# A two-layer spiking and gated network on one core: the recurrence's product written over its PSUM bank, and new instruction orders for all engines

## The chip, the cores and the metric

The kernel runs on one core of a Trainium2 chip. A core has five engines that matter here, each with its own queue that it works off strictly in order: TensorE (PE, matrix products into PSUM), VectorE (DVE), ScalarE (ACT), GpSimd (POOL) and SyncE (SP, which issues the transfers). They meet only at semaphores. The metric is the device time of one execution in microseconds. Three runs of the kernel before gave 676.83, 680.20 and 680.25 us; the median is 680.2.

## The reference

The input `x` has 32 sequences of 256 tokens with 128 channels. Cut to what matters:

```python
def _L0_attn_ref(x, ...):
    x = x + lif(time_mix(layer_norm(x, ln1_s, ln1_b), ...))        # spikes after a recurrence over time
    x = x + lif(channel_mix(layer_norm(x, ln2_s, ln2_b), ...))     # spikes after a gated relu-square layer
    return x

def wkv(w_decay, u, k, v):                                         # inside time_mix
    def step(carry, kv_t):
        ...
        y = (A * p + Bc * vt) / (A * q + Bc)
        return ((A2 * p + B2 * vt, A2 * q + B2, no2), y)

def _L0_ffn_ref(x, ...):
    h = silu(tlin(x, w1)) * tlin(x, w2)
    h = gelu(tlin(h, h1)); h = gelu(tlin(h, h2))
    return tlin(h, w3)

x = x + _layernorm(_L0_attn_ref(_layernorm(x), ...))
x = x + _layernorm(_L0_ffn_ref(_layernorm(x), ...))
```

## The kernel before

The 32 sequences are worked in 16 groups of two, so a group has 512 tokens. Most of the work is on tiles of 128 partitions by 512 values: channels on partitions, the tokens of a group along them. A group passes five sections.

1. Normalise, transpose (`turn_1`, `z_1`), subtract the token before (`shift_1` on GpSimd), blend three inputs (`mix_1`), multiply by Wk, Wv and Wr (`k_product` into bank `p_k`, `v_product` into `p_v`, `r_product_1` into `p_m[0]`). The recurrence is done with scans on VectorE: `maximum` (running maximum over `p_k`), `excess`, `bounds`, exponentials on ScalarE, then `terms(1)` = B2 * v and `sum_over_time(0)` (the scan of p), `sum_over_time(1)` (the scan of q), `weighted_sum` on GpSimd, `denominator`, `numerator`, and `log`, `inverse`, `ratio`, `ratio_end`. `out_product` multiplies by Wo.
2. Spikes: `fire(0)` compares with the threshold and counts, `fired_sum(0)` sums the count on TensorE, `fired_flag(0)` on VectorE copies it out, and `neurons(0)` on GpSimd steps the neurons one by one only where the flag is not zero. `spikes_turned(0)` transposes the spikes back.
3. The channel section: `norm_2`, `turn_2`, `z_2`, `shift_2`, `mix_2`, products `r_product`, `channel_k`, relu, square, `channel_v`, then `neuron_input_2`, `fire(1)`, `fired_flag(1)`, `neurons(1)`, `spikes_turned(1)`, `residual_3`.
4. The gated layer: `norm_4`, `turn_4`, `f0`, four `to_gate` and four `to_value` products with SiLU and `swiglu`, two `hidden` layers of sixteen block products each with `gelu`, and `last_product`. Every activation of this layer is split in a high part (`high` on ScalarE) and a remainder (`low` on VectorE or GpSimd), and each block is multiplied twice.
5. `output_scaled`, `turn_5`, `output_tokens`, a last normalisation (`variance(5)`, `norm_5`) and `residual_5` on GpSimd, and the store.

Five groups are in flight at a time. The program of each engine is written out as turns: in turn i the group i is normalised for the first time, i-1 is in the recurrence, i-2 in its spikes and the channel section, i-3 behind it, i-4 in the gated layer. Three hand-written orders per engine (`first_turn`, `turn`, `last_turn`) are called for turns by `schedule`. TensorE's program is written twice, for weights whose remainder is zero and for others; the choice, a branch on a value loaded from memory, comes after the first turns, behind `channel_k` of the first group. The weights' high parts and remainders (`high_weights`, `low_weights`, `rest_weights`, `rest_max`, `rest_sum`, `rest_flag`) are made in the opening.

PSUM has eight banks: `p_turn` for all transposes, `p_spk`, `p_k`, `p_v`, two `p_m`, two `p_f`. `p_v` takes the v product and two of the four gate products (`to_gate` 1 and 3). TensorE waits, with `after`, until the readers of a bank are done. The lines of the recurrence that the change touches are, before:

```python
dve.tensor_tensor(flat(bv[:, n]), flat(factors[:, 2 + n]), p_v[:, :], ALU.mult).then_inc(s_bv[n], 1)   # terms
new = factors[:, 3] if n else bv[:, 1]                                                                  # sum_over_time
dve.tensor_tensor_scan(pq[:, n, b, 1:T + 1], factors[:, 1, b], new[:, b], 0.0, ALU.mult, ALU.add)
after(pe, s_bv[0], g.n + 2)      # to_gate, m == 1
after(pe, s_bv[1], g.n + 2)
```

## Time and profile before

| | us |
|---|---|
| median of three runs | 680.2 |
| profiled execution | 681.2 |
| its span on the core | 679.1 |
| TensorE busy | 589.6 (87%) |
| VectorE busy | 550.5 (81%) |
| ScalarE busy | 537.6 (79%) |
| GpSimd busy | 439.8 (65%) |

All durations come from the one profiled execution. TensorE's busy time is modelled: matmuls overlap, and the pitch of a row of them is shorter than the time that each is shown with. Idle time of an engine that is waited for by nobody costs nothing, so the shares alone decide nothing: the kernel has an opening in which no engine is full, twelve turns in which TensorE is busy nearly all the time, and an end. The reading below goes by these stretches, then by the waits of one engine, then by single rows.

### The profile page before, as it was taken

How to read it: one execution, taken by the hardware profiler on the slowest of the kernel's cores; microseconds unless marked ns; L12 is line 12 of the kernel's file. 1: busy time of each engine (PE TensorE's matmuls, PEld its weight loads, DVE VectorE, ACT ScalarE, POOL GpSimd, SP SyncE). 2: the span in 40 equal slices, each digit the busy share in tenths (PEclk: the TensorE clock that was granted, in tenths of full speed). 3: DMA queues.
4: the chain of work that ended last, by engine and by line, in shares of the span. 5: the costliest groups of instructions: out<-in, count | busy, mean ns of one | idle time of the engine just before them, and what ended most of it. 6: DMA issues, size and time to landing. Idle time of an engine off the chain costs nothing. (4 is left out here: it accounts for less than half of the span.)

```text
span 679.1 us, 10282 instructions
## 1 busy us (share of the span) xinstructions
PE 589.6 (87%) x2241; PEld 365.0 (54%) x2241; DVE 550.5 (81%) x1532; ACT 537.6 (79%) x849; POOL 439.8 (65%) x576
## 2 busy tenths in 40 slices
PE   1247579999999999999999999999999999989883
PEld 0022236566565657565666656565756566656562
DVE  2865768989898998989898989899898989775631
ACT  4846367998989797979799898979797979858672
POOL 4323454687868686876878786868687784744452
PEclk9857779999999999999999999999999999999997
DMA  6100010001010100101010101010010101000000
GB/s 221 62 18 17 0 32 17 16 17 32 15 33 16 32 0 17 32 17 32 16 33 16 32 18 31 17 32 1 18 31 1 33 0 32 17 0 17 1 16 15
DMA packets 26560, 17.05 MB, mean 25 GB/s; under 512 B 1152, under 2 KB 25728, under 8 KB 26240
## 3 DMA queue, kind: packets, MB, share of 16 engines
q1 hardware_dynamic: 26496, 16.34, 8.0%
q8 instruction: 23, 0.38, 0.2%
q14 instruction: 41, 0.34, 0.2%
HBM read 12.14 MB, written 4.19 MB: 24 GB/s over the span
## 5 line engine op out<-in xcount | busy, mean ns | idle before, releaser
L774 ACT ACTIVATE hid<-p_f,scale 128x512 f32<-128x512 f32 x128 | 88.0, 688 | 64.5 <-PE p_f L1715 64.1
L1715 PE MATMUL p_f<-a_lo,w_hi 128*128 128x512 f32 x320 | 133.1, 416 | 2.8 <-DVE a_lo L293 1.7
L1715 PE MATMUL p_f<-a_hi,w_hi 128*128 128x512 f32 x320 | 125.9, 393 | 0.0
L1715 PE MATMUL p_f<-b_lo,w_hi 128*128 128x512 f32 x256 | 111.8, 437 | 3.5 <-DVE b_lo L293 2.3
L1715 PE MATMUL p_f<-b_hi,w_hi 128*128 128x512 f32 x256 | 100.6, 393 | 0.0
L421 POOL TENSOR_TENSOR rstd<-var,minus_half 128x4 f32<-128x4 f32 x64 | 91.0, 1422 | 2.5
L768 ACT ACTIVATE a_hi<-hid 128x512 fp32r<-128x512 f32 x128 | 79.1, 628 | 2.9 <-DVE hid L1254 1.5
L437 POOL TENSOR_TENSOR nd<-factors,pq 128x512 f32<-128x512 f32 x32 | 39.3, 1229 | 58.6 <-DVE pq L1121 58.6
L293 DVE TENSOR_TENSOR a_lo<-hid,a_hi 128x512 fp32r<-128x512 f32 x96 | 63.8, 689 | 11.2 <-ACT a_hi L768 10.9
L1715 PEld LDWEIGHTS p_f<-a_lo,w_hi 128*128 128x128 f32 x320 | 60.3, 188 | 22.5 <-issue 8.1
L293 POOL TENSOR_TENSOR b_lo<-hid,b_hi 128x512 fp32r<-128x512 f32 x32 | 46.8, 1478 | 34.2 <-ACT b_hi L768 29.4
L1700 PE MATMUL p_m<-kk,mix 128*128 128x512 f32 x128 | 64.1, 607 | 3.6 <-issue 3.6
L1684 PE MATMUL p_m<-mixed,mix 128*128 128x512 f32 x128 | 65.3, 613 | 1.5 <-DVE kk L1200 1.5
L1715 PEld LDWEIGHTS p_f<-a_hi,w_hi 128*128 128x128 f32 x320 | 60.3, 189 | 9.9 <-issue 0.5
L1715 PEld LDWEIGHTS p_f<-b_lo,w_hi 128*128 128x128 f32 x256 | 48.0, 188 | 30.6 <-issue 20.2
L408 POOL TENSOR_TENSOR var<-mv,eps_row 128x4 f32<-128x4 f32 x64 | 23.0, 359 | 58.3 <-DVE mv L1049 58.2
L1715 PEld LDWEIGHTS p_f<-b_hi,w_hi 128*128 128x128 f32 x256 | 48.2, 188 | 13.0 <-issue 3.1
L1521 PE MATMUL p_turn<-ident,n 128*128 128x128 f32 x192 | 32.2, 293 | 25.0 <-ACT n L657 12.2
L1521 PEld LDWEIGHTS p_turn<-ident,n 128*128 128x128 f32 x192 | 22.9, 147 | 54.3 <-DVE n L1064 25.0
L1715 PE MATMUL p_f<-f_lo,w_hi 128*128 128x512 f32 x64 | 39.9, 623 | 8.5 <-ACT gate L755 7.1
L293 POOL TENSOR_TENSOR a_lo<-hid,a_hi 128x512 fp32r<-128x512 f32 x32 | 41.8, 1305 | 7.7 <-ACT a_hi L768 7.7
L511 POOL TENSOR_SCALAR f_out<-f_out,rstd,shift 128x128 f32<-128x128 f32 x64 | 43.2, 689 | 0.2 <-POOL shift L503 0.2
(141 smaller groups left out, 1457.3 us busy)
## 6 DMA issues: line engine op xcount, KB each, us to landing
xa<-in_x SPq DMA_DIRECT2D x16, 256.0 KB, 2.8
xb<-in_x SPq DMA_DIRECT2D x16, 256.0 KB, 2.9
out<-y_out SPq DMA_DIRECT2D x16, 256.0 KB, 3.3
kk<-in_ffn SPq DMA_DIRECT2D x1, 1024.0 KB, 7.6
hid<-in_ffn SPq DMA_DIRECT2D x1, 1024.0 KB, 10.0
mix<-in_mix SPq DMA_DIRECT2D x1, 512.0 KB, 6.3
gate<-in_ffn SPq DMA_DIRECT2D x1, 512.0 KB, 4.5
mix<-in_mix SPq DMA_DIRECT2D x1, 320.0 KB, 3.9
```

The costliest lines, as they stand in the source:

```text
L293: eng.tensor_tensor(lo[:, m], hid[:, m], hi[:, m].bitcast(F32), ALU.subtract).then_inc(s_lo[layer][m], 1)
L408: pool.tensor_tensor(var[n][:, :], mv[n][:, :, 1], eps_row[:, :], ALU.add).then_inc(s_var[n], 1)
L421: pool.tensor_tensor(rstds[n][:, :], var[n][:, :], minus_half[:, 0], ALU.pow).then_inc(s_rstd[n], 1)
L437: pool.tensor_tensor(nd[:, n], factors[:, 0], pq[:, n, :, 0:T], ALU.mult).then_inc(s_apq, 1)
L511: last = pool.tensor_scalar(f_out[:, j], f_out[:, j], rstd5[:, j:j + 1], shift5[:, j:j + 1], ALU.mult, ALU.add)
L768: act.activation(dst[:, m], hid[:, m], ACT.Copy).then_inc(s_hi[layer], 1)
L774: act.activation(hid[:, m], p_f[m % 2][:, :], ACT.Gelu, scale=scale[:, 1 + layer, m:m + 1]).then_inc(s_gelu[layer], 1)
L1521: last = pe.transpose(p_turn[:, j * P:(j + 1) * P], tiles[:, j], ident[:, :])
L1684: pe.matmul(p_m[m % 2][:, :], mix[:, MIX["fWk"] + m], flat(mixed2[:, 1]), start=True, stop=True).then_inc(s_fk, 1)
L1700: last = pe.matmul(p_m[0][:, :], mix[:, MIX["fWv"] + m], kk[:, m], start=(m == 0), stop=(m == HB - 1))
L1715: last = pe.matmul(out_, w[:, b], x[:, k], start=(k == 0 and t == 0), stop=(k == n - 1 and t == len(terms) - 1))
```

## The change

Two things change. First, `terms(1)` writes its product over the values of `p_v` in PSUM, and `sum_over_time(0)` scans from there; `bv` keeps only the product of `terms(0)`. `terms(0)` has to come before `terms(1)` now, which a wait enforces. Second, the orders of all engines are laid anew: per engine one `opening` (up to the first groups' gated layer), one `turn` that is looped for i = 5 to 12, and one `ending`, each a plain list of steps. TensorE's waits on banks stand in these lists between the steps, no longer inside the steps, and its branch on the weights comes between `opening` and `onset`. The steps themselves are the same.

```diff
@@ terms
+                if n == 1:
+                    dve.wait_ge(s_bv[0], g.n + 1)
-                dve.tensor_tensor(flat(bv[:, n]), flat(factors[:, 2 + n]), p_v[:, :], ALU.mult).then_inc(s_bv[n], 1)
+                dve.tensor_tensor(p_v[:, :] if n else flat(bv[:, :, :]), flat(factors[:, 2 + n]), p_v[:, :], ALU.mult).then_inc(s_bv[n], 1)
@@ sum_over_time
-                new = factors[:, 3] if n else bv[:, 1]
+                new = factors[:, 3] if n else p_v[:, :].rearrange("p (b t) -> p b t", b=NB)
@@ numerator
-                dve.tensor_tensor(nd[:, 0], nd[:, 0], bv[:, 0], ALU.add).then_inc(s_num, 1)
+                dve.tensor_tensor(nd[:, 0], nd[:, 0], bv[:, :, :], ALU.add).then_inc(s_num, 1)
@@ all engines
-            schedule(first_turn, turn, last_turn)
+            opening()
+            for i in range(FIRST, LAST + 1):
+                turn(groups(i))
+            ending()
@@ tensor, the looped turn
+                    after(pe, s_f_cm, g[4].n)
+                    to_gate(g[3], 0)
+                    after(pe, s_f0_hi, g[3].n)
+                    after(pe, s_f0_lo, g[3].n)
+                    turn_5(g[4])
...
+                    after(pe, s_pq, g[1].n, 2, 2)
+                    to_gate(g[3], 1)
@@ gpsimd, the looped turn
+                shift_1(g[0])
+                norm_5(g[4])
+                neurons(1, g[2])
+                neurons(0, g[1])
```

VectorE in an even turn, around the two copies of the spike counts (`fired_all1` of the older group, `fired_all0` of the younger; `mixed1` is `mix_1`, `spikes` is `fire`, `b_lo` is `low(2)`). Before:

```order
L1206 SCALAR_TENSOR_TENSOR h_in1<-tanh_r2,p_m0 128x512
L293 TENSOR_TENSOR a_lo<-hid,a_hi 128x512 x2
L1155 TENSOR_SCALAR spikes1,fired1<-h_in1 128x512
L1162 COPY fired_all1<-p_m0 1x1
L1155 TENSOR_SCALAR spikes0,fired0<-p_k 128x512
L1080 SCALAR_TENSOR_TENSOR mixed1<-d1,vec,z1 128x512
L1162 COPY fired_all0<-p_m0 1x1
L1212 TENSOR_TENSOR x3<-p_spk,x2 128x512
```

The same place now:

```order
L1590 SCALAR_TENSOR_TENSOR h_in1<-tanh_r2,p_m0 128x512
L1539 TENSOR_SCALAR spikes0,fired0<-p_k 128x512
L1539 TENSOR_SCALAR spikes1,fired1<-h_in1 128x512
L1462 SCALAR_TENSOR_TENSOR mixed1<-d1,vec,z1 128x512
L1546 COPY fired_all1<-p_m0 1x1
L1431 BN_AGGR mv1<-bn1 128x2 x4
L1462 SCALAR_TENSOR_TENSOR mixed1<-d1,vec,z1 128x512 x2
L287 TENSOR_TENSOR b_lo<-hid,b_hi 128x512
L1546 COPY fired_all0<-p_m0 1x1
L1596 TENSOR_TENSOR x3<-p_spk,x2 128x512
```

The younger group's `fire` and all three `mix_1` now stand ahead of or between the two copies, with `moments_1` and a `low(2)`.

ScalarE in the opening, first group (`w_rest` marks the passes over the weights' remainders, `y<-nd` is `log`, `y<-y` is `inverse`). Before:

```order
L704 ACTIVATE factors<-factors 128x1024
L643 ACTIVATE w_hi<-gate 128x1024
L649 ACTIVATE kk,w_rest<-w_lo 128x2048
L643 ACTIVATE w_hi<-f_cm 128x512
L649 ACTIVATE hid,w_rest<-w_lo 128x2048
L649 ACTIVATE gate,w_rest<-w_lo 128x1024
L649 ACTIVATE f_cm,w_rest<-w_lo 128x512
L710 ACTIVATE y<-nd 128x512
L714 ACTIVATE y<-y 128x512
L657 ACTIVATE n1<-xa,nmr1,rstd1 128x128 x4
```

The same place now:

```order
L832 ACTIVATE factors<-factors 128x1024
L829 ACTIVATE factors<-factors 128x1024
L785 ACTIVATE n1<-xa,nmr1,rstd1 128x128 x4
L838 ACTIVATE y<-nd 128x512
L842 ACTIVATE y<-y 128x512
L777 ACTIVATE hid,w_rest<-w_lo 128x2048
L794 ACTIVATE z1<-p_turn,vec 128x2x256
L848 ACTIVATE h_in0<-p_k 128x512
L777 ACTIVATE kk,w_rest<-w_lo 128x2048
```

The passes over the remainders moved behind `inverse`, and the second group's `norm_1` (`n1`) ahead of `log`.

ScalarE at the last group (`f_cm` is `output_scaled` and `f_out` is `output_tokens` of the group before, `gate` is SiLU). Before:

```order
L747 ACTIVATE f0_hi<-p_turn 128x512
L782 ACTIVATE f_cm<-p_f0,vec 128x512
L787 ACTIVATE f_out<-p_turn 128x512
L693 ACT_TABLE_LOAD
L755 ACTIVATE gate<-p_f0,scale 128x512
```

The same place now:

```order
L875 ACTIVATE f0_hi<-p_turn 128x512
L821 ACT_TABLE_LOAD
L910 ACTIVATE f_cm<-p_f0,vec 128x512
L883 ACTIVATE gate<-p_f0,scale 128x512
```

The table load moved ahead of `output_scaled`, and `output_tokens` behind the SiLU steps.

## Rows read from the trace of the kernel before

**Rows 1.** Stretches: length; busy PE, PEld, DVE, ACT, POOL; clock; DMA; GB/s

```profile
0.00:99.45 99.45, 47.67 (x98) 19.41 (x98) 62.70 (x166) 53.73 (x77) 38.39 (x69) 0.74 0.18 60
...
320.52:357.26 36.74, 35.55 (x142) 22.45 (x140) 33.56 (x96) 32.28 (x53) 27.98 (x36) 1.00 0.08 23
...
541.00:578.79 37.79, 35.93 (x142) 22.50 (x141) 33.77 (x90) 32.75 (x53) 25.05 (x31) 1.00 0.05 15
...
642.30:679.10 36.80, 22.31 (x90) 15.42 (x88) 10.87 (x28) 19.14 (x28) 15.61 (x24) 0.87 0.05 15
```

**Rows 2.** Waits of PE, ten turns from 136.64: us in total, times, longest

```profile
PE p_f L1715 <- ACT gate L755: 4.5, 10, 0.5
PE p_m L1646 <- DVE mixed L1192: 3.2, 10, 0.3
PE p_turn L1521 <- DVE n L1064: 2.1, 10, 0.2
```

**Rows 3.** Waits of DVE in the same ten turns

```profile
DVE fired_all L1162 <- PE p_m L1616: 25.8, 20, 2.2
```

**Rows 4.** Timeline of DVE in one turn: start, us, operation, [idle before]

```profile
331.94 0.15 DVE L1162 COPY fired_all<-p_m 1x1 f32<-1x1 f32 x1 [2.16 <-PE p_m L1616]
...
342.29 0.75 DVE L1080 SCALAR_TENSOR_TENSOR mixed<-d,vec,z 128x512 f32<-128x512 f32 x1
...
347.02 1.29 DVE L293 TENSOR_TENSOR a_lo<-hid,a_hi 128x512 fp32r<-128x512 f32 x2
...
349.60 1.67 DVE L1064 TENSOR_SCALAR n<-xres,mv,rstd 128x128 f32<-128x128 f32 x4
```

**Rows 5.** Groups of DVE by form: count, busy us, mean ns

```profile
L1110 DVE TENSOR_TENSOR bv<-factors,p_v 128x512 f32<-128x512 f32 x32 | 21.3, 666 | 0.0
L1121 DVE TENSOR_TENSOR_SCAN pq<-factors,bv 128x256 f32<-128x256 f32 x32 | 20.3, 675 | 0.0
...
L1087 DVE TENSOR_TENSOR_SCAN o<-decay_row,p_k 128x256 f32<-128x256 f32 x32 | 19.7, 659 | 1.2 <-PE p_k L1555 1.2
```

**Rows 6.** Timelines of DVE, ACT and PE in the opening

```profile
31.28 0.69 DVE L1128 TENSOR_TENSOR nd<-nd,factors 128x512 f32<-128x512 f32 x1 [0.55 <-POOL nd L437]
...
70.13 0.69 DVE L1206 SCALAR_TENSOR_TENSOR h_in<-tanh_r,p_m 128x512 f32<-128x512 f32 x1 [2.94 <-PE p_m L1700]
...
34.45 0.61 ACT L710 ACTIVATE y<-nd 128x512 f32<-128x512 f32 x1
...
37.13 2.05 PE L1595 MATMUL p_k<-yr,mix 128*128 128x512 f32 x2 [2.05 <-issue]
...
42.52 0.61 PE L1632 MATMUL p_spk<-ident,spikes 128*128 128x128 bf16 x4 [2.29 <-POOLq L476]
...
64.72 5.37 PE L1700 MATMUL p_m<-kk,mix 128*128 128x512 f32 x8 [3.59 <-issue]
...
96.71 0.47 PE L1715 MATMUL p_f<-f_lo,w_hi 128*128 128x512 f32 x1 [1.34 <-DVE f_lo L1243]
```

**Rows 7.** Timeline at the last group

```profile
641.75 0.39 PE L1715 MATMUL p_f<-f_hi,w_hi 128*128 128x512 f32 x1
...
642.32 1.28 ACT L693 ACT_TABLE_LOAD   x1
...
643.61 0.69 ACT L755 ACTIVATE gate<-p_f,scale 128x512 f32<-128x512 f32 x1
...
648.39 0.48 PE L1715 MATMUL p_f<-a_lo,w_hi 128*128 128x512 f32 x1 [1.02 <-POOL a_lo L293]
```

**Rows 8.** Timelines of POOL, ACT and PE around the spikes of one turn

```profile
327.91 2.81 POOL L511 TENSOR_SCALAR f_out<-f_out,rstd,shift 128x128 f32<-128x128 f32 x4
330.69 1.04 POOL L442 TENSOR_TENSOR d<-z 128x512 f32<-128x512 f32 x1
...
328.28 0.76 ACT L666 ACTIVATE z<-p_turn,vec 128x512 f32<-128x512 f32 x1
...
333.72 0.38 PE L1632 MATMUL p_spk<-ident,spikes 128*128 128x128 bf16 x4
```

More of the change, by code:

```diff
@@ L1003, in _ @@
+            opening()
+            for i in range(FIRST, LAST + 1):
+                turn(groups(i))
+            ending()
         @block.vector
@@ L1513, in _ @@
+            opening()
+            for i in range(FIRST, LAST + 1):
+                turn(groups(i))
+            ending()
         @block.tensor
@@ L1516, in _, with program @@
             pe.wait_ge(s_vec, 4)
-            def program(general, **turns):
+            def program(general, first):
                 def turned(n, g, tiles):
@@ L2063, in _ @@
+                if first:
+                    opening()
+                else:
+                    onset()
+                    for i in range(FIRST, LAST + 1):
+                        turn(groups(i))
+                    ending()
+            program(False, True)
             for k in range(len(parts)):
```

2829 lines of the change are left out of this document (1848 added, 981 removed).

## Prediction

> **What bounds the kernel now.** I read first the busy time by stretch, then the waits of one engine at a time inside the even stretch, then the timelines at the places where a wait sits. The stretches are cut at the load of the SiLU table, which ScalarE makes once per group. [rows 1] show three parts: an opening of 99.45 us until the first of them, with TensorE busy 47.67 us at a mean granted clock of 0.74; twelve even turns, of which one stands there (36.74 us; TensorE 35.55, VectorE 33.56, ScalarE 32.28, GpSimd 27.98 busy); and 138.1 us behind 541.00, of which the first turn takes 37.79 and the last group alone 36.80, with TensorE busy for 22.31 of them. In an even turn TensorE bounds: it is idle 1.19 us, VectorE 3.18, ScalarE 4.46. [rows 2] say where TensorE's 1.19 go, over ten turns: 4.5 us for the SiLU gate, 3.2 us for `mix_2`, 2.1 us for the normalised tokens of `norm_4`, so 0.98 a turn out of 1.19. Two of these three are VectorE's lateness. Yet VectorE itself stands still 2.58 us a turn at `fired_flag`, for a sum on TensorE [rows 3]; most of it is one gap of 2.16 us [rows 4]. VectorE waits early in the turn and is late at its end: that can be mended by order alone. The opening and the end are bound by chains of single steps, not by any engine's work.
>
> **The arithmetic of the recurrence.** `terms(1)` writes its product into the PSUM bank instead of SBUF, and the two scans of `sum_over_time(0)` read it there. No instruction is added or removed: per group one 128x512 product and two 128x256 scans change an operand. The product with an operand already in PSUM takes 666 ns, the scan with both operands in SBUF 675, the scan with one in PSUM (the `maximum` scan of `p_k`) 659 [rows 5]. The nearest row therefore gives -16 ns a scan, 32 x 16 ns = 0.5 us in all; a VectorE write into PSUM has no row here. From below, 0.5 us gained; from above, if product and scans each became slower by what separates a `mix_1` (0.75 us [rows 4]) from this product, about 80 ns x 48 = 3.8 us. I take nought, because the scan row with PSUM is the nearest.
> [...]
> The bank `p_v` now stays taken until the scan ends (`to_gate(1)` waits for `s_pq`, no longer for `s_bv`). Before, the order was scan then `terms(0)`; now both products precede the scan. In either order the last of the same instructions frees the bank, so this costs nothing; if the scan were last by a whole product more, 0.66 us a turn.
>
> **The even turns.** TensorE's order hardly moves: the output transposes go behind the first gate product, one `channel_v` goes behind the value products. What moves is VectorE's. Into the gap at `fired_flag(1)` come `fire(0)` and one `mix_1`, and between the two flags `moments_1`, two more `mix_1` and a `low(2)`. So 2 x 0.74 us of `mix_1` leave the path from the `maximum` scan to `mix_2`, and one `low(3)` (half of the 1.29 us pair) goes from before `norm_4` to behind it [rows 4]. I walked the new order through one turn with these durations: `mix_2` can come only as early as `z_2` and `shift_2` allow, about 0.3 us earlier than now; `norm_4`, which starts at 349.60, is free some 0.8 us earlier; then ScalarE, which runs without a gap from `z_2` to `output_scaled`, becomes what the first gate product waits for. The walk gives a turn between 35.1 and 36.1, depending on how the short ScalarE gaps round. Bounds: nothing gained, if ScalarE takes over at once, and 1.19 us, if every idle moment of TensorE went. I take 0.65, somewhat over half of the ceiling and the late end of the walk: 12 x 0.65 = 7.8 us, bounds 0 and 14.3.
>
> **The opening.** Four steps. (a) `log` of the first group ran at 34.45, with four passes over the weights' remainders ahead of it on ScalarE; the denominator that it needs was complete at 31.97 [rows 6]. The passes now stand behind `inverse`. That is 2.5 us, and `stats_1` of the next group no longer holds up the first `mix_1` (0.9 us): the out product goes from 37.13 to about 33.7. (b) TensorE then stood 2.29 us for the spikes at 42.52 [rows 6], since GpSimd had the next group's `shift_1` ahead of `neurons`, and that waited for `z_1`. The transposes and `z_1` of that group now come before the out product: 2.3 us. (c) In front of the channel products TensorE stood 3.59 us on its own instruction stream, at the branch on the weights [rows 6]. The branch moves to behind the first `turn_4`. Here I count 1 us, as the squares on ScalarE are late there too; the new place costs up to 3.6 us at the first gate product. (d) Between `neuron_input_2` at 70.13 and the first gate product at 96.71 [rows 6] the new order brings `norm_4` of the first group ahead of work for the third: some 5 us, of which (c) takes back 3.6. In all 3.4 + 2.3 + 1 + 5 - 3.6 is 8.1; I take 7.2, because one new wait (the weights' maximum sits on TensorE before `v_product`) may hold 1 us. Bounds: 2.5, if only (a) holds, and 11, if the branch hides behind other waits.
>
> **The end.** For the last group the first gate product was ready at 642.14, but SiLU began at 643.61 behind the table load at 642.32 [rows 7]. Now the table is loaded ahead of `output_scaled`, and `turn_5` of the group before goes behind the gate products: 1.5 to 1.9 us. GpSimd's `low(1)` then stood behind the variance of the group before, and TensorE waited 1.02 us for it [rows 7]; it now stands ahead. Together 2.4 us at the last group. The three stretches before it have the same pattern with shorter waits; I take 1.6 us for all three. Sum 4.0, bounds 0 and 7.
>
> **The sum.** The profiled execution took 681.2 us (span 679.1). 681.2 - 7.8 - 7.2 - 4.0 = 662.2. It lies 1.0 us above the median of the runs, 680.2, so on the median the forecast is 661.2. With all lower bounds 681.2 - 0 - 2.5 - 0 - 1.0 = 677.7; with all upper ones 681.2 - 14.3 - 11 - 7 - 1.0 = 647.9.
>
> **Rivals.** *ScalarE takes over.* The turn stays at 36.74, as ScalarE's run up to `output_scaled` is the new chain; opening and end keep their gain: 680.2 - 7.2 - 4.0 = 669.0. For it: ScalarE has 32.28 us in a turn [rows 1] and waits only for products. Against: two of TensorE's waits are for VectorE [rows 2]. Chance 0.2.
> *The orders buy nothing measurable.* The opening's gain is given back as a wait of the second and third group, whose steps were moved behind the first's, and the even turns are as long as before: only the end is left, 680.2 - 2.4 = 677.8. Within 0.5% (676.8 to 683.6), which is about what a measurement of this kernel can tell from no change. For it: the twelve turns set the pace whatever starts earlier. Chance 0.1.
> *Slower: GpSimd between `shift_1` and `neurons`.* `norm_5` now stands directly ahead of `neurons(1)`, and TensorE needs the spikes in order. `z_1` ends at 329.04, `shift_1` takes 1.04, `norm_5` took 2.81 beside VectorE [rows 8]: 332.9, and the spike transposes are due at 333.72, so 0.8 us are left for `neurons`. The four `norm_5` instructions now run beside `fire` and `mix_1` of VectorE. If each is held for a 0.75 us instruction, four take 4.8 us and the turn grows by 2.0: 680.2 - 7.2 - 4.0 + 12 x 2.0 = 693. It decides the sign from 0.93 us a turn (11.2 / 12). Against: in the even turn before, 2.81 us were stretched already, and the transposes waited on GpSimd nowhere there [rows 2]. Chance 0.08.
> [...]
>
> **How the numbers follow.** Forecast 661.2 with its neighbourhood (648 to 668): 0.62. ScalarE takes over, 669.0: 0.2. Nothing measurable, 677.8: 0.1. Slower, 693: 0.08. The range goes from 649 to 677: it takes in the forecast, the first rival and nearly all of the sum's bounds. Faster by over 0.5% is forecast and first rival, 0.82; within 0.5% 0.1; slower 0.08.
>
> **What would show it.** Right: the first SiLU table load near 92 us instead of 99.45; even turns of 36.1; `fired_flag`'s wait under 1 us a turn; scans on `p_v` at 0.66 us; the last SiLU directly behind its gate product. Wrong: a wait of TensorE for the spikes on GpSimd in each turn, a wait of the first gate product for the scan of `p_v`, product or scans on `p_v` above 0.75 us, or a first table load later than 97 us.

## The result: 671.0 us, and the profile of the changed kernel

The changed kernel took 671.03 us in the median of four runs (669.68 to 673.51), the kernel before 678.52 us on the same chip: a ratio of 0.9895, 95% interval 0.9847 to 0.9942. It is faster by about 1%, and the time lies inside the range, but the gain is 7.5 us where 19 were forecast. The profiled execution is the slowest of the four (673.5 us, span 671.6), so stretches below are compared trace with trace: 679.1 before, 671.6 after.

The stretches, cut as in [rows 1] at the load of the SiLU table (columns as there; two even turns stand here, because there are two kinds now):

```profile
0.00:89.48 89.48, 43.65 (x94) 17.54 (x95) 64.07 (x171) 53.52 (x77) 43.14 (x72) 0.81 0.20 66
202.01:239.52 37.51, 35.52 (x142) 22.58 (x140) 34.88 (x96) 32.35 (x52) 24.11 (x35) 1.00 0.07 22
277.05:313.55 36.50, 35.51 (x142) 22.59 (x140) 34.00 (x96) 32.37 (x52) 24.55 (x35) 1.00 0.08 23
537.76:574.99 37.23, 35.34 (x143) 22.71 (x141) 34.69 (x89) 32.57 (x54) 20.63 (x27) 1.00 0.05 15
633.34:671.60 38.26, 24.48 (x102) 17.12 (x100) 11.70 (x30) 20.03 (x30) 15.25 (x25) 0.89 0.05 14
```

The opening fell from 99.45 to 89.48 us (-9.97, forecast -7.2), the part from the thirteenth table load on from 138.1 to 133.84 (-4.3, forecast -4.0). The twelve even turns between them grew from 441.55 to 448.28 us: +6.7 where -7.8 were forecast. That is more than the whole miss: opening and end together gained 3 us more than forecast. (The last table load is no clean cut any more: it now comes ahead of the first gate product, as planned.)

Eight of the twelve turns belong to the looped order; these are looked at from here on. Their table loads lie at 173.36 and 467.49 before (294.1 us, 36.77 each) and at 164.50 and 461.99 after (297.5 us). They give 3.4 of the 6.7 us; the two turns ahead of them grew by 1.1 us and the two behind them by 2.3, and these four belong to the written-out opening and end. Five of the eight take 37.5 us, three 36.5 to 36.8. TensorE's busy time is the same in both kinds (35.5), VectorE's is not: 34.88 against 34.00, with the same 96 instructions.

The waits of TensorE over these eight turns (us in total, times, longest):

```profile
PE p_f L2233 <- DVE b_lo L287: 5.5, 5, 1.1
PE p_v L2233 <- DVE pq L1505: 2.9, 8, 0.4
PE p_f L2233 <- DVE hid L1638: 2.3, 8, 0.5
PE p_m L2202 <- DVE mixed L1576: 1.3, 8, 0.2
```

The waits of [rows 2] for the gate and for `norm_4` are gone. In their place stand three waits for VectorE: 1.1 us for `low(2)` (`b_lo`) in exactly the five long turns, 0.36 us in each turn for the scan of `p_v` ahead of the second gate product, 0.29 us for `swiglu` (`hid`). VectorE's own wait of [rows 3] has gone as intended, from 2.58 to 0.29 us a turn:

```profile
DVE fired_all L1546 <- PE p_m L2186: 2.3, 8, 0.3
```

The forms of VectorE that answer to [rows 5] (count, busy us, mean ns, idle before), and `low(2)`:

```profile
L287 DVE TENSOR_TENSOR b_lo<-hid,b_hi 128x512 fp32r<-128x512 f32 x32 | 28.2, 882 | 9.7 <-ACT b_hi L896 9.7
...
L1505 DVE TENSOR_TENSOR_SCAN pq<-factors,p_v 128x256 f32<-128x256 f32 x32 | 20.2, 674 | 1.6
...
L1494 DVE TENSOR_TENSOR p_v<-factors,p_v 128x512 f32<-128x512 f32 x16 | 11.1, 692 | 1.3
...
L1494 DVE TENSOR_TENSOR bv<-factors,p_v 128x512 f32<-128x512 f32 x16 | 10.8, 678 | 0.0
```

The scan takes 674 ns from PSUM as it took 675 from SBUF, the product into the bank 692 instead of 666 to 678. `b_lo` went from 679 ns in the kernel before to 882. Its rows in a long turn (first three lines) and in a short one (last two), from the timelines of GpSimd, VectorE and TensorE (start, us, operation, [idle before]):

```profile
219.55 1.32 POOL L507 TENSOR_TENSOR y_out<-f_out,xres 128x512 f32<-128x512 f32 x1
...
219.59 1.83 DVE L287 TENSOR_TENSOR b_lo<-hid,b_hi 128x512 fp32r<-128x512 f32 x1
...
221.56 0.48 PE L2233 MATMUL p_f<-b_lo,w_hi 128*128 128x512 f32 x1 [1.10 <-DVE b_lo L287]
...
294.65 0.81 DVE L287 TENSOR_TENSOR b_lo<-hid,b_hi 128x512 fp32r<-128x512 f32 x1
...
294.86 1.75 POOL L507 TENSOR_TENSOR y_out<-f_out,xres 128x512 f32<-128x512 f32 x1
```

In the long turn GpSimd's `residual_5` (`y_out`) starts 0.04 us before VectorE's `low(2,3)`; the latter then takes 1.83 us, which is the 1.28 us that `residual_5` still runs and some 0.55 of its own. In the short turn `low(2,3)` starts first, and `residual_5` takes 1.75 us. Which of the two goes first decides whether TensorE waits 1.1 us. At a distance of 0.02 us the recorded starts do not tell which it will be: in the turns with `residual_5` at 182.08 and 257.12 it leads by 0.02 us and goes first, and at 443.03, in the last of the eight turns, it leads by as much, but `low(2,3)` goes first (0.67 us) and `residual_5` takes 1.86 us.

### The profile page after: what moved, and what is told of

It is laid out like the page before. It is cut to its first block and busy times, and to the rows that moved or that the text cites. A ratio compares the mean times of both kernels' runs of the same rounds, so it can differ in the third digit from the quotient of the medians.

```text
span 671.6 us, 9752 instructions
## 1 busy us (share of the span) xinstructions
PE 585.3 (87%) x2241; PEld 365.9 (54%) x2241; DVE 561.4 (84%) x1532; ACT 537.4 (80%) x849; POOL 401.7 (60%) x576
## 5 line engine op out<-in xcount | busy, mean ns | idle before, releaser
L287 DVE TENSOR_TENSOR a_lo<-hid,a_hi 128x512 fp32r<-128x512 f32 x96 | 65.8, 705 | 8.7 <-ACT a_hi L896 7.8
L410 POOL TENSOR_TENSOR rstd<-var,minus_half 128x4 f32<-128x4 f32 x64 | 69.3, 1087 | 1.6
L287 POOL TENSOR_TENSOR a_lo<-hid,a_hi 128x512 fp32r<-128x512 f32 x32 | 49.4, 1544 | 33.2 <-ACT a_hi L896 33.0
L287 POOL TENSOR_TENSOR b_lo<-hid,b_hi 128x512 fp32r<-128x512 f32 x32 | 42.3, 1323 | 37.8 <-DVE fired_all L1546 23.5
L2142 PE MATMUL p_turn<-ident,n 128*128 128x128 f32 x192 | 30.6, 284 | 29.1 <-ACT n L785 21.0
L1462 DVE SCALAR_TENSOR_TENSOR mixed<-d,vec,z 128x512 f32<-128x512 f32 x48 | 35.8, 768 | 11.7 <-POOL d L431 11.7
L397 POOL TENSOR_TENSOR var<-mv,eps_row 128x4 f32<-128x4 f32 x64 | 15.4, 246 | 48.1 <-DVE mv L1431 48.1
L418 POOL TENSOR_SCALAR x<-xa,neg_mean,rstd 128x128 f32<-128x128 f32 x64 | 40.0, 637 | 0.2 <-POOL rstd L406 0.2
```

What stands on the lines that cost most here:

```text
L287: eng.tensor_tensor(lo[:, m], hid[:, m], hi[:, m].bitcast(F32), ALU.subtract).then_inc(s_lo[layer][m], 1)
L397: pool.tensor_tensor(var[n][:, :], mv[n][:, :, 1], eps_row[:, :], ALU.add).then_inc(s_var[n], 1)
L410: pool.tensor_tensor(rstds[n][:, :], var[n][:, :], minus_half[:, 0], ALU.pow).then_inc(s_rstd[n], 1)
L418: last = pool.tensor_scalar(out_[:, j], in_[:, j], neg_mean[n][:, j:j + 1], rstd[:, j:j + 1], ALU.add, ALU.mult)
L1462: dve.scalar_tensor_tensor(mixed1[:, n], d1[:, :, :], col(("tmk", "tmv", "tmr")[n]), z1[:, :, 0:T], ALU.mult, ALU.add).then_inc(s_mixed1, 1)
L2142: last = pe.transpose(p_turn[:, j * P:(j + 1) * P], tiles[:, j], ident[:, :])
```

## The experiments

Two questions: do the long turns come from this collision, and why does a turn without it still take 36.5 us where the walk gave 36.1. Times are medians; a ratio stands with its 95% interval, against the kernel before on the same chip (678.5 us for the changed kernel, 679.7 to 680.1 us for the others). "Eight turns" are the looped ones, in the one profiled execution of each run. The runs x8 to x10, x13, x14, x18 and x19 leave out parts of the work, so that their output is not the layer's; they serve only to find what bounds a turn.

| run | time, us | ratio to before | eight turns, us |
|---|---|---|---|
| before | 678.5 | | 294.1 |
| changed | 671.0 | 0.9895 (0.9847 to 0.9942) | 297.5 |
| x5_yield | 667.6 | 0.9828 (0.9801 to 0.9855) | 291.8 |
| x6_collide | 692.3 | 1.0192 (1.0167 to 1.0217) | 302.4 |
| x2_resid | 679.3 | 0.9998 (0.9985 to 1.0010) | 303.3 |
| x4_arith | 684.7 | 1.0072 (1.0048 to 1.0095) | 296.9 |
| x1_sbuf | 672.8 | 0.9911 (0.9884 to 0.9938) | 295.2 |
| x7_yield_sbuf | 669.8 | 0.9871 (0.9843 to 0.9898) | 291.8 |
| x3_both | 683.2 | 1.0060 (1.0039 to 1.0082) | 304.8 |
| x8_less_act | 666.1 | 0.9809 (0.9777 to 0.9840) | 291.8 |
| x9_less_dve | 667.8 | 0.9830 (0.9796 to 0.9864) | 291.6 |
| x10_sbuf_less_act | 668.7 | 0.9851 (0.9816 to 0.9886) | 291.7 |
| x13_less_both | 665.7 | 0.9794 (0.9780 to 0.9808) | 291.4 |
| x14_less_pool | 666.8 | 0.9818 (0.9791 to 0.9844) | 291.8 |
| x18_all | 664.7 | 0.9796 (0.9751 to 0.9842) | 291.2 |
| x19_den | 664.1 | 0.9788 (0.9742 to 0.9834) | 289.4 |
| x15_late5 | 676.7 | 0.9943 (0.9929 to 0.9958) | 300.3 |
| x16_late5_sbuf | 678.0 | 0.9979 (0.9967 to 0.9990) | 300.1 |
| x11_two_yields | 667.5 | 0.9829 (0.9803 to 0.9854) | 291.7 |
| x12_log_late | 671.9 | 0.9894 (0.9864 to 0.9925) | 295.2 |

### The collision, taken out and put in

**x5_yield.** `residual_5` lets `low(2,3)` go first:

```diff
@@ changed kernel, GpSimd, looped turn
                 low(2, g[3], 2)
+                pool.wait_ge(s_lo[2][3], g[3].n + 1)
                 residual_5(g[4])
```

> The changed kernel with one wait more in GpSimd's even turn: residual_5 keeps its place, but begins only when low(2,3) of VectorE is done. Theory of the collision (who comes first at the SBUF decides, and in five of eight turns residual_5 came first by some 40 ns): low(2,3) takes 0.7 to 0.8 us in every turn, TensorE's wait of 1.1 us for it is gone, and residual_5, which took 1.75 us in the short turns because it waited itself, ends where it ended in those. No turn of 37.5 us is left among the eight, they take 292.5 us instead of 297.5, and the whole time is 666 instead of 671. Rival (GpSimd's chain behind residual_5 is the bound, as x2_resid hints, where its delay came back as a wait for weighted_sum): the eight turns take 303 and the whole 677 or more.

667.62 us, and all runs between 667.35 and 667.88. TensorE's wait for `b_lo` is no longer among its waits over the eight turns, and no turn of 37.5 us is left among them. First the waits, then the form of VectorE:

```profile
PE p_v L2234 <- DVE pq L1506: 2.9, 8, 0.4
PE p_f L2234 <- DVE hid L1639: 2.3, 8, 0.5
PE p_m L2203 <- DVE mixed L1577: 1.3, 8, 0.2
```

```profile
L287 DVE TENSOR_TENSOR b_lo<-hid,b_hi 128x512 fp32r<-128x512 f32 x32 | 22.5, 703 | 9.5 <-ACT b_hi L897 9.5
```

The eight turns fall by 5.7 us, the expected 5. An added wait made the kernel faster: this version beats both kernels, by 3.4 us the changed one.

**x6_collide.** The reverse: in the kernel before, only this line of GpSimd's order goes where the change put it.

```diff
@@ kernel before, GpSimd, turn
                 if on[0]:
                     shift_1(g[0])
-                if on[4]:
-                    residual_5(g[4])
...
                     low(2, g[3], 2)
+                if on[4]:
+                    residual_5(g[4])
```

> The kernel before with one line of GpSimd's even turn moved as the change moved it: residual_5 from ahead of neurons to behind low(2,2). In the kernel before, low(2,2) ends at 337.81 and low(2,3) of VectorE begins at 337.93, so residual_5 would come first by 0.1 us. Theory of the collision: low(2,3) grows from 0.67 to about 1.8 us, TensorE waits about 1.1 us for it, a turn grows from 36.75 to 37.3 to 37.8 us, and the whole time by 6 to 12 us to 685 to 691. Rival (the collision needs the other moves of the change too, or is hidden): 679 +- 1.5, and low(2,3) as before.

692.33 us; each looped turn grows by 1.03 us. The form of `b_lo` has 1063 ns on the mean over all 32 instructions instead of 679, and TensorE waits 1.1 us for it in each of the eight turns:

```profile
L293 DVE TENSOR_TENSOR b_lo<-hid,b_hi 128x512 fp32r<-128x512 f32 x32 | 34.0, 1063 | 7.8 <-ACT b_hi L768 7.8
```

```profile
PE p_f L1715 <- DVE b_lo L293: 8.8, 8, 1.1
```

So the move of one GpSimd instruction to where it meets `low(2,3)` costs 12.5 us, and the collision is shown from both sides.

**x2_resid.** Moving `residual_5` further back instead of letting it wait:

```diff
@@ changed kernel, GpSimd, looped turn
-                residual_5(g[4])
                 variance(2, g[1])
                 variance(3, g[2])
                 rstd(2, g[1])
+                residual_5(g[4])
                 rstd(3, g[2])
```

> The changed kernel with one line of GpSimd's even turn moved: residual_5 stands behind rstd(2) instead of directly behind low(2,2). Theory of the collision (in the long turns residual_5 of GpSimd starts some 40 ns before low(2,3) of VectorE, which then takes 1.83 us instead of 0.68, and TensorE waits 1.1 us for it): low(2,3) takes 0.7 us in each turn, TensorE's wait of 1.1 us for it is gone, the five long turns of 37.5 us become 36.5 us, eight turns take 292.5 us instead of 297.5, the whole 666 instead of 671. Rival (the long turns come from the spikes' flag, which GpSimd waits for ahead of low(2,0), or from VectorE's amount of work): low(2,3) stays long or another of VectorE's instructions gets long in its place, turns of 37.5 stay, 671 +- 1.

679.31 us, 8 us slower than the changed kernel. The collision with `low(2,3)` was gone (`b_lo` 703 ns), but GpSimd ran later, and an instruction of 0.20 us (`neg_mean`) came beside three VectorE instructions with two SBUF inputs in a row and took 1.92 us. Its row on GpSimd, and the wait of TensorE that came of it over the eight turns:

```profile
308.76 1.92 POOL L399 TENSOR_TENSOR neg_mean<-mv,minus_one 128x4 f32<-128x4 f32 x1
```

```profile
PE p_v L2233 <- DVE pq L1505: 11.7, 8, 1.6
```

The expectation was right on the place and wrong on the time: the collision had moved to a dearer place.

### The arithmetic and the bank

**x4_arith.** The new arithmetic alone, in the old orders:

```diff
@@ kernel before, with the change's terms, sum_over_time and numerator; VectorE, turn
+                    terms(g[1], 0)
                     terms(g[1], 1)
                     denominator(g[1])
                     sum_over_time(g[1], 0)
-                    terms(g[1], 0)
```

> The kernel before with the new arithmetic alone: the second product is written over p_v and scanned there, the first product goes ahead of it, and TensorE waits for the scan where it waited for the products; all other orders are those of before. If the arithmetic is worth nought, as predicted: the time of before, 678.5 +- 1.5, turns of 36.75 us, scans of 0.67 us; in the old order a product stood behind the scans, so the bank is released no later than before. Rival (PSUM costs VectorE time): product or scans above 0.75 us, up to 3.8 us more in all. Rival (the bank): a wait of TensorE for the scan takes the place of the 0.45 us wait for the gate, and the turn grows by what the scan is later.

684.70 us, 4.9 us more than the kernel before, a turn 37.1 instead of 36.77. The instructions cost what was forecast (product 696 and 670 ns, scan 671), yet a turn is 0.34 us longer, since the product that must now go first pushes `denominator` back: ScalarE waits 0.24 us a turn for it, which it did not before, and TensorE's wait for the gate [rows 2] grows from 0.45 to 0.80 us. Over eight turns, ScalarE and TensorE:

```profile
ACT y L710 <- DVE nd L1130: 1.9, 8, 0.2
```

```profile
PE p_f L1715 <- ACT gate L755: 6.4, 8, 0.8
```

The changed kernel escapes this: its order has `denominator` ahead of both products.

**x1_sbuf** and **x7_yield_sbuf**: the old arithmetic in the new orders, without and with the added wait of x5_yield.

```diff
@@ changed kernel, terms and sum_over_time as before the change; TensorE, all orders
-                    after(pe, s_pq, g[1].n, 2, 2)
+                    after(pe, s_bv[1], g[1].n)
                     to_gate(g[3], 1)
```

> The changed kernel with the old arithmetic: the second product goes to SBUF again and is scanned from there, and the second gate product waits for the two products on the bank, no longer for the scan. Theory of the bank (the bank p_v is held for two scans, 1.26 us, longer than it need be, and TensorE pays 0.36 us of that in each turn): the wait of TensorE for the scan of p_v (0.4 us a turn in the changed kernel) is gone, an undisturbed turn falls from 36.5 to about 36.1, and the whole time by 12 x 0.36 = 4 us, from 671 to 667. Rival (ScalarE takes over): the same 0.4 us come back as a wait for the SiLU gate, as in the kernel before, and the time stays at 671 +- 1. Rival (the product into PSUM and the scans from it are slower): product 692 -> 670 ns, scans 674 -> 675 ns, 0.4 us in all.

> x5_yield with the old arithmetic (second product to SBUF, bank released by the products). x1_sbuf showed short turns of 36.4 to 36.6 us, TensorE's wait for the scan replaced by waits for the gate and for swiglu. If ScalarE's run up to the gate bounds an undisturbed turn, the eight turns take 291.5 to 292.5 us and the time is that of x5_yield within 1.5 us. If the bank bounds it, 4 us less than x5_yield.

x1_sbuf took 672.8 us, so the 4 us of the bank did not come; three of its eight turns are long by the collision. The wait for the scan goes, and in its place come waits for `swiglu` and for the gate; without the collision the eight turns are 291.8 us with and without the early release. TensorE in x7_yield_sbuf:

```profile
PE p_f L2234 <- DVE hid L1639: 3.0, 8, 0.6
PE p_f L2234 <- ACT gate L884: 2.2, 8, 0.3
```

So the bank is not what holds the turn. The time is 2.2 us above x5_yield, all of it outside the looped turns: the first table load is 1.1 us later (90.88 against 89.79), the end 0.8 us longer. In these orders a scan from SBUF takes 728 ns on the mean, from PSUM 674 (the form of x1_sbuf):

```profile
L1505 DVE TENSOR_TENSOR_SCAN pq<-factors,bv 128x256 f32<-128x256 f32 x32 | 21.9, 728 | 1.6
```

The 54 ns are no price of each scan. In x1_sbuf a pair of scans takes 1.26 to 1.28 us, but for three pairs of 2.20, 1.74 and 1.44 us, and beside each of these three GpSimd has an instruction; they make 1.6 of the 1.7 us that 32 scans lost. The first of the three, VectorE and GpSimd in x1_sbuf, and the same place of VectorE in the changed kernel, where the same GpSimd instruction starts at 28.35 and the scans are not held:

```profile
28.26 2.20 DVE L1505 TENSOR_TENSOR_SCAN pq<-factors,bv 128x256 f32<-128x256 f32 x2
28.30 1.61 POOL L426 TENSOR_TENSOR nd<-factors,pq 128x512 f32<-128x512 f32 x1 [1.45 <-DVE pq L1505]
...
28.30 1.26 DVE L1505 TENSOR_TENSOR_SCAN pq<-factors,p_v 128x256 f32<-128x256 f32 x2
```

**x3_both** is x1_sbuf and x2_resid together.

> Both edits at once: old arithmetic with the bank released by the products, and residual_5 behind rstd(2). If both theories hold and their gains lie at different places of the turn, a turn takes about 36.1 us, eight turns 289, and the whole time is 671 - 5 - 4 = 662, which is the forecast of the prediction. If only the collision counts 666, if only the bank 667; if neither 671.

683.22 us. With the bank released early the 1.46 us a turn of x2_resid turn up chiefly as a wait for the gate of ScalarE (7.6 us in eight turns), since `log` waits for the late `denominator`. Neither gain showed.

### What holds a turn without the collision

The rival of the prediction was that ScalarE takes over. **x8_less_act** takes work from ScalarE behind the exponentials, **x9_less_dve** from VectorE ahead of the scans, **x10_sbuf_less_act** joins x7 and x8.

```diff
@@ x5_yield, ScalarE (x8_less_act): output_scaled, f0, output_tokens
-                act.activation(f_cm[:, 0], p_f[0][:, :], ACT.Copy, scale=col("w3_s"))
+                act.activation(f_cm[:, 0, 0:64], p_f[0][:, 0:64], ACT.Copy, scale=col("w3_s"))
...
@@ x5_yield, split_low (x9_less_dve)
+            n = 64 if layer == 3 and m else N
-            eng.tensor_tensor(lo[:, m], hid[:, m], hi[:, m].bitcast(F32), ALU.subtract)
+            eng.tensor_tensor(lo[:, m, 0:n], hid[:, m, 0:n], hi[:, m, 0:n].bitcast(F32), ALU.subtract)
```

> x5_yield with less work on ScalarE: output_scaled and f0 do 64 of 512 columns, output_tokens 128 of 512, from the second group on; the output is not the layer's. That is some 1.1 us a turn in the run that ends in the SiLU gate. If ScalarE's run bounds an undisturbed turn, it falls from 36.5 to between 35.6 and 36.0 us and the eight turns to 285 to 288. If VectorE or the bank bounds it, turns stay at 36.5 and the wait of TensorE for the scan of p_v stays at 0.4 us.

> x5_yield with less work on VectorE: low(3,1), low(3,2) and low(3,3) do 64 of 512 columns; the output is not the layer's. That is some 1.6 us a turn, at the end of VectorE's run ahead of the scans and the gate. If VectorE's run bounds an undisturbed turn (x8_less_act left it at 36.47 us with 1.1 us less on ScalarE, and the wait for the scan of p_v stayed), the turn falls to between 35.7 and 36.1 us, the eight turns from 291.8 to 286 to 289, and TensorE's wait of 0.4 us for the scan of p_v is gone. Rival (ScalarE and VectorE end together, so that taking work from one shows the other): at most 0.1 us a turn, 291 for the eight, and a wait for the gate in place of that for the scan.

> x7_yield_sbuf (bank released by the products) with the reduced work on ScalarE of x8_less_act; the output is not the layer's. In x7 the wait for the scan was replaced by waits for the gate (0.3 us) and for swiglu (0.4 us), in x8 it stayed. If the bank and ScalarE's run end within 0.1 us of each other and both must go, the turn falls here from 36.47 to about 36.1 us and the eight turns to 289. If VectorE's run is the bound whatever the bank and ScalarE do, 36.4 to 36.5 us and a wait for swiglu of VectorE remains.

None of the three moved the turn: 291.8, 291.6, 291.7 us. ScalarE therefore is not the bound by its amount of work, and the rival falls; nor is VectorE ahead of the scan. In x9 VectorE stood idle for what it had saved: 1.2 us a turn in front of the first scan, where x5_yield has 0.3 (the profile names no releaser; the exponentials end there), and 0.6 us in front of an earlier instruction:

```profile
DVE pq L1507 <- issue: 8.3, 7, 1.2
```

**x13_less_both** shortens ScalarE ahead of the exponentials as well (`high(3,1..3)` on 64 columns).

> x9_less_dve, and on ScalarE high(3,1), high(3,2) and high(3,3), which run ahead of the exponentials, also do 64 of 512 columns; a part of the feed-forward's third input is left out. Theory of the chain: the undisturbed turn of 36.4 us is bound by exps on ScalarE (end at 308.38), the scan behind it on VectorE (start at 308.47) and VectorE's 7.4 us from there to swiglu. VectorE alone (x9) and ScalarE behind the exponentials alone (x8) changed nothing, since VectorE is free for the scan only 0.27 us before the exponentials end. With both shortened ahead of that point by more than 1 us the scan starts about 1 us earlier, and the turn falls from 36.4 to 35.6 to 36.0 us, the eight turns from 291.8 to 285 to 288. Rival (TensorE with its own order, or GpSimd, bounds the turn): 291 to 292 again.

291.4 us: missed. The scan still waits 1.2 us, as ScalarE now stands idle in front of `tanh_2` for `r_product`, that is for `mix_2`. From ScalarE's timeline:

```profile
226.72 0.60 ACT L861 ACTIVATE tanh_r<-p_m 128x512 f32<-128x512 f32 x1 [0.28 <-PE p_m L2205]
```

**x14_less_pool** shortens what leads to `mix_2` on GpSimd (`residual_5` on a quarter).

> x5_yield with residual_5 of GpSimd on one quarter of its columns from the second group on (a part of the output is left out): about 0.9 us less on GpSimd between low(2,3) of VectorE and rstd(2). In x13_less_both the scan still waited 1.2 us, now for tanh_2, which waited for r_product, that is for mix_2: behind mix_2 come r_product, tanh_2, the table load, exps (2.1 us), the scan. Theory of the ring (one chain through all engines, from the spikes over add_1, low(2,3), residual_5 and rstd(2) on GpSimd, norm_2, z_2, shift_2, mix_2, tanh_2, exps, scan, swiglu back to TensorE's products and the spikes, sets the turn, and work beside it counts nothing): VectorE's wait of 0.44 us for rstd(2) goes, mix_2 and all behind it come 0.44 us earlier, the undisturbed turn falls from 36.4 to 35.9 to 36.1 us, the eight turns from 291.8 to 288 to 289, 664.5 instead of 667.6. Rival (TensorE's own order is the bound, or mix_2 waits for something else): 291 to 292 again.

291.8 us: missed too. VectorE's wait for `rstd(2)` went, but `mix_2` waited for `shift_2` instead, which waits for `z_2`, and `z_2` follows `turn_2`. That transpose starts without a wait, where it stands in TensorE's order. VectorE's wait, and TensorE's row:

```profile
DVE mixed L1578 <- POOL d L436: 4.4, 8, 0.6
```

```profile
223.50 0.60 PE L2144 MATMUL p_turn<-ident,n 128*128 128x128 f32 x4
```

This gave the last theory: one chain from `turn_2` over `z_2`, `shift_2`, `mix_2`, `r_product`, `tanh_2`, the table load, the exponentials, the scan, `weighted_sum`, `denominator`, `terms` and the scan of `p_v` to the gated layer's products. TensorE works on between, in order, and closes the ring at the next `turn_2`. No cut so far had shortened a link of it. **x18_all** makes all cuts beside the chain at once (and puts `z_2` ahead of `under(1)`); **x19_den** shortens one link, from 0.69 to 0.22 us.

```diff
@@ x5_yield, VectorE (x19_den)
-                dve.tensor_tensor(nd[:, 1], nd[:, 1], factors[:, 2], ALU.add).then_inc(s_den, 1)
+                n = 32 if g.n else T
+                dve.tensor_tensor(nd[:, 1, :, 0:n], nd[:, 1, :, 0:n], factors[:, 2, :, 0:n], ALU.add).then_inc(s_den, 1)
```

> All cuts beside the chain at once: bank released by the products, low(3,1..3) and high(3,1..3) on 64 of 512 columns, output_scaled and f0 on 64, output_tokens and residual_5 on a quarter, and z_2 one place earlier on ScalarE; parts of the feed-forward and of the output are left out. Theory of the ties (several stretches of ScalarE, VectorE and GpSimd end within 0.5 us of each other, so each cut alone only showed the next): with all of them cut the turn falls from 36.4 to 35.6 to 36.0 us, the eight turns to 285 to 288. Theory of the chain from turn_2 (in x14_less_pool turn_2 starts at its own place in TensorE's order, without a wait, and z_2, shift_2, mix_2, r_product, tanh_2, table load, exps, scan, weighted_sum, denominator, terms, scan and the gate's products follow one another; none of the cuts shortens one of these): 36.2 to 36.5 us, eight turns 290 to 292, as in all cuts before.

> x5_yield with one instruction of the chain itself shortened: denominator on 64 of its 512 columns from the second group on (the quotient is wrong in the others). It is 0.69 us on VectorE between weighted_sum and the two terms. Theory of the chain from turn_2: terms, the scan from p_v and ScalarE's log come 0.4 us earlier, TensorE's wait for the scan (0.36 us) goes, and the turn falls from 36.4 to between 35.9 and 36.2 us, the eight turns from 291.8 to 287 to 290. Rival (TensorE's own work, or another ring that the chain does not pass, holds the turn): 291 to 292, with a wait of TensorE of the same size at another place.

x18_all stayed at 291.2 us, with 1.5, 1.7 and 2.7 us less busy time a turn on VectorE, ScalarE and GpSimd than x7_yield_sbuf; TensorE's waits of 0.36 and 0.29 us became one of 0.69 us for `swiglu`. x19_den came down to 289.4, an ordinary turn from 36.36 to 36.09, and both waits went, as the chain has it. TensorE in x18_all, then in x19_den:

```profile
PE p_f L2239 <- DVE hid L1644: 5.5, 8, 0.9
```

```profile
PE p_m L2204 <- DVE mixed L1578: 1.3, 8, 0.2
PE p_turn L2264 <- DVE f_lo L1629: 0.3, 1, 0.3
PE p_f L2235 <- POOL b_lo L287: 0.2, 1, 0.2
PE p_f L2235 <- DVE hid L1640: 0.2, 1, 0.2
```

0.47 us off one link of the chain bought 0.3 us a turn; some 6 us beside it bought less than 0.1. Only one link was shortened. That the links ahead of it belong to the chain is read from x18_all: with the work beside them cut, the next engine waits at these handovers in seven or all of the eight turns (`z_2` for `turn_2`, `mix_2` for `shift_2`, `tanh_2` for `r_product`, the scan for the exponentials, this last again without a named releaser). ScalarE and VectorE there:

```profile
ACT z L856 <- PE p_turn L2148: 6.0, 8, 0.8
DVE mixed L1582 <- POOL d L437: 4.4, 8, 0.6
ACT tanh_r L862 <- PE p_m L2208: 2.3, 8, 0.3
DVE pq L1511 <- issue: 8.1, 7, 1.2
```

That the ring closes over TensorE's order from the gate's products to the next `turn_2` is argued, not shown. A rival is left as well: `denominator` also belongs to VectorE's own run from the first scan to `swiglu`, and no run cut that run at another place.

**x15_late5** and **x16_late5_sbuf** move `stats_5` and `moments_5` behind `swiglu(1)`, in x5_yield and x7_yield_sbuf, to bring `swiglu` forward with nothing left out.

```diff
@@ VectorE, looped turn
                 sum_over_time(g[1], 0)
-                stats_5(g[4])
-                moments_5(g[4])
                 swiglu(g[3], 0)
                 swiglu(g[3], 1)
+                stats_5(g[4])
+                moments_5(g[4])
```

> x5_yield with stats_5 and moments_5 of VectorE's even turn moved behind swiglu(1); nothing is left out. They are 1.2 us inside the 7.4 us of VectorE that lead from the scan to swiglu. Theory of the chain: TensorE's wait for swiglu (0.3 us a turn) goes, the wait for the scan of p_v (0.36 us) stays, as the bank is released no earlier; turn 36.1 to 36.3 us, the eight turns 289 to 290.5, the time 665.5 to 667. Rival (the bank's release sets the pace alone): 291.8 and 667.6 again.

> The same move in x7_yield_sbuf, where the bank is released by the products: neither the wait for the scan nor that for swiglu should be left, only that for the gate of ScalarE (0.3 us a turn). Theory of the chain: turn 35.9 to 36.2 us, the eight turns 287 to 289.5, 3 to 4 us less than x7_yield_sbuf, so 666. Rival (ScalarE's gate takes the whole): 291.8 and 669.8 again.

Both lost 9 and 8 us. `swiglu` then waits 0.94 us for its own products, and what was moved stands in front of `numerator` and `ratio_end`; TensorE waits 1.2 us a turn for the latter (x15_late5, eight turns):

```profile
PE p_k L2182 <- DVE yr L1529: 9.8, 8, 1.5
```

The statistics had filled a gap. The chain did not tell where else to put them.

### Opening and end

**x12_log_late** undoes a part of step (a) of the opening, in the changed kernel: two of the passes over the remainders go ahead of `log` again.

```diff
@@ changed kernel, ScalarE, opening
+                rest_weights(1)
+                rest_weights(0)
                 log(G[0])
                 inverse(G[0])
-                rest_weights(1)
...
-                rest_weights(0)
```

> The changed kernel with a part of its new opening undone: the two largest passes over the weights' remainders (2.1 us each) go ahead of the first group's log again, as in the kernel before. By the prediction's step (a), log was 2.5 us later than its denominator for that reason alone, and 3.4 us at the out product: out product from 33.77 to 37 or 38, the first SiLU table load from 89.5 to between 92.5 and 93.5, and 671 becomes 674 to 675. Rival (the opening is bound elsewhere, by GpSimd's spikes and the weights' branch): first table load at 89.5 to 90.5, 671 to 672.

`log` ran 2.0 us later (32.39 instead of 30.36), the out product 0.8 (34.57 instead of 33.77), and at the first table load nothing was left (89.25; in ten runs with the new opening unchanged it lies between 88.1 and 89.9). So the 3 to 4 us that were expected at the table load did not come. TensorE in the changed kernel, then in x12_log_late, at the branch:

```profile
85.08 2.04 PE L2218 MATMUL p_m<-kk,mix 128*128 128x512 f32 x2 [4.73 <-issue]
```

```profile
85.21 2.04 PE L2218 MATMUL p_m<-kk,mix 128*128 128x512 f32 x2 [4.47 <-issue]
```

**x11_two_yields** adds a second wait of x5's kind in the written-out end, where `low(3,0)` on GpSimd starts 0.16 us before `residual_3`, which takes 2.17 us instead of 1.14.

```diff
@@ x5_yield, GpSimd, ending
                 rstd(3, G[12])
+                pool.wait_ge(s_xres, G[12].n + 1)
                 low(3, G[11], 0)
```

> x5_yield with the same kind of wait once more, in the written-out end: low(3,0) of the group 11 on GpSimd waits for residual_3 of group 12 on VectorE. In x5_yield, low(3,0) starts at 516.41, and residual_3 at 516.57 takes 2.17 us instead of 1.14; mix_2 is late and TensorE waits 1.2 us for it. If that wait is the collision's, residual_3 takes 1.15 us, TensorE's 1.2 us shrink to 0.4 or less, that turn goes from 38.24 to about 37.4, and the time from 667.6 to 666.8. Rival (something else of the end takes the place): 667.6 +- 0.4.

667.49 us, that turn 38.04 instead of 38.24: no gain that can be told from none. `residual_3` came down to 1.13 us, but `bounds` behind it went from 0.45 to 1.29 us, now beside GpSimd's `shift_2`, which starts 0.03 us ahead of it, and TensorE's wait for `mix_2` only fell from 1.2 to 1.0 us. The collision had moved to the next pair.

## Why the prediction was right or wrong

**The arithmetic: right as to the instructions.** The scan is the same (674 against 675 ns), the product 14 to 26 ns dearer: 0.2 to 0.4 us in 16. Not foreseen: x4_arith lost 0.34 us a turn by the order that the arithmetic enforces, and scanning from PSUM is worth 2.2 us in the new orders (x7_yield_sbuf against x5_yield): from SBUF, three pairs of scans there meet GpSimd and take 2.20, 1.74 and 1.44 us, where a pair from PSUM takes 1.25 to 1.27 in x5_yield. "In either order the last of the same instructions frees the bank, so this costs nothing" held in its result (x7_yield_sbuf), though the wait for it does appear.

**The opening: right in size, by other steps.** -9.97 against -7.2, inside the bounds 2.5 to 11. Step (a): out product 37.13 to 33.77, as forecast (33.7). Step (b): 0.7 instead of 2.3; TensorE still stands 1.57 us for the spikes (at 38.44, where it stood 2.29 [rows 6]). Step (c) brought more than the 1 us that was counted: from the first `channel_k` to the first `channel_v` it took 9.9 us (54.79 to 64.72) and takes 5.6 now (49.14 to 54.75). At the first `channel_v` 10.0 us are gained, at `neuron_input_2`, 70.13 to 60.36, 9.8. From there to the table load it took 29.3 us before and takes 29.1 now: step (d), 5 us less 3.6, brought 0.2, as TensorE now stands 4.73 us at the branch's new place. x12_log_late shows that gains upstream can be swallowed there, 2.0 us at `log` wholly, so the steps do not simply add. TensorE at the first `channel_v`:

```profile
54.75 1.02 PE L2218 MATMUL p_m<-kk,mix 128*128 128x512 f32 x2
```

**The end: -4.3 against -4.0, but in part by shifted work.** At the last group the first SiLU now starts at 636.15, directly behind its product, and the wait for GpSimd's `low(1)` [rows 7] shrank from 1.02 to 0.65 us. Against that, 2.3 us were lost in the two even turns ahead of it, which belong to the written-out end; TensorE's busy time there is 36.2 and 36.1 us instead of 35.6, so about half of it is work that stood elsewhere before. With these two turns counted in, the written-out end gained 2.0 us.

**The even turns: wrong, and this is the step that failed.** The prediction put -0.65 us a turn, "bounds 0 and 14.3", with no bound on the other side, from a walk of the new order through one turn. It measured +0.42 in the looped turns. Two things were missing.

First the collision, +0.7 us a turn on the mean (5.7 us in eight). The walk followed VectorE's order ("What moves is VectorE's") and costed GpSimd's at nothing there: it does not speak of `residual_5`, which the change puts behind `low(2,2)`, beside VectorE's `low(2,3)`. Before, `residual_5` ran its 1.31 us from the end of VectorE's gap of 2.16 us [rows 4] on, beside the copy of a flag and `fire(0)`, which reads PSUM and took 0.69 us, and met only the start of a `mix_1` (0.86 us, where the one of [rows 4] takes 0.75). GpSimd and VectorE in the kernel before:

```profile
331.69 1.31 POOL L518 TENSOR_TENSOR y_out<-f_out,xres 128x512 f32<-128x512 f32 x1
...
332.07 0.69 DVE L1155 TENSOR_SCALAR_CACHE_REDUCE spikes<-p_k 128x512 bf16<-128x512 f32 x1
...
332.69 0.86 DVE L1080 SCALAR_TENSOR_TENSOR mixed<-d,vec,z 128x512 f32<-128x512 f32 x1
```

The filling of the gap was not the fault: x6_collide leaves the gap as it was, moves `residual_5` alone, and loses 12.5 us. The prediction looked for such a hold, but for `norm_5` beside `fire` and `mix_1`, at an estimated 4.8 us; that place stayed harmless: `norm_5` takes 2.19 us now, it took 2.81 [rows 8]. At `residual_5` and `low(2,3)` the later one is the long one: 1.83 us for `low(2,3)` where `residual_5` goes first, 1.75 for `residual_5` where `low(2,3)` does. Where they do not overlap (x5_yield, at 218.20 and 218.95) they take 0.67 and 1.30.

Second the size of the gain without the collision: -0.30 us a turn (x5_yield, 294.1 to 291.8 in eight) instead of -0.65. The walk took the waits of [rows 2] for VectorE as curable by order and ScalarE's run as the next limit. What limits, as far as x18_all and x19_den show it, is a chain over four engines. In x5_yield and in every cut but x19_den TensorE's waits changed their name and kept a sum near 0.9 us a turn; x19_den brought them to 0.25. With the collision gone, the twelve turns of x5_yield still take 442.0 us, as before the change (441.6), since the four written-out ones are 2.8 us longer.

**The rivals.** ScalarE taking over (669.0) was near the measured time by accident: x8_less_act shows that ScalarE's work is not the bound. GpSimd slowing the turn down was the right kind of rival with the wrong pair and a chance of 0.08; its 2.0 us a turn, from a `norm_5` of 4.8 us, stands in no run. Of the signs named, "first table load near 92" came better (89.5), "`fired_flag` under 1 us" held (0.29), "scans at 0.66" came as 0.67, "turns of 36.1" did not come, and one sign against, a wait for the scan of `p_v`, did come in each turn, though at the second gate product and not the first.

## What to carry to other kernels

A new order moves the instructions of every engine, and one that cost next to nothing at its old place can collide at its new one (`residual_5` lengthened a `mix_1` by 0.1 us at the old one; moved alone, in x6_collide, it cost 12.5 us): for everything that is moved, list what VectorE and GpSimd each do there, and which of their operands lie in SBUF (the pair of scans at 28.3 took 2.20 us from SBUF and 1.26 from PSUM, each beside the same GpSimd instruction). Where two such instructions meet within hundredths of a microsecond, a wait that fixes who goes first can be worth more than any order (here 3.4 us for one line). And where taking work away from one engine after another changes only the name of the wait (here some 6 us of work for less than 0.1 us a turn), suspect a chain through several of them: test it by shortening one of its links (here 0.47 us of one for 0.3 us a turn).

## What the runs showed of the hardware

A GpSimd instruction of 0.20 us on 128x4 values took 1.92 us beside three VectorE instructions with two SBUF inputs that followed one another closely (x2_resid): it is recorded from 308.76 to 310.68, the first two from 308.80 on with 1.28 us, the third from 310.01 on as one of two that took 1.26 us together, so it ended about when the third did. Two executions of the same turn in one run differ by 1 us (36.5 and 37.5) by which of two instructions goes first, and with recorded starts 0.02 us apart it went either way. With that choice taken away (x5_yield) the five runs lie within 0.53 us, where the four of the changed kernel spread over 3.8; it is not the only source of spread, as x7_yield_sbuf and x15_late5, with the same wait, spread over 2.9 and 3.0. A scan with both inputs in SBUF took as long as one with an input in PSUM (1.27 us a pair in x1_sbuf, 1.26 in the changed kernel) where GpSimd stood still, and up to 2.20 us beside a GpSimd instruction (x1_sbuf). In one place an instruction with a single tile from SBUF seems to have been held too: `bounds`, which reads 128x512 values and a column, took 1.29 us instead of 0.45 beside a GpSimd instruction that had started 0.03 us earlier (x11_two_yields).
